# A first stage and a tail written anew in an eight-layer kernel on one core

## The reference, cut to what matters

```python
def _mlstm_cell(q, k, v, ...):            # first layer; q = layernorm(x), k = v = ctx
    ig = einsum('bsf,hf->bsh', concat([q, k, v]), igate_w) + igate_b      # 4 heads
    fg = einsum('bsf,hf->bsh', concat([q, k, v]), fgate_w) + fgate_b
    log_fg = log_sigmoid(fg);  cs = cumsum(log_fg)                        # over 64 tokens
    log_D = cs - shifted(cs).T + ig.T, below the diagonal, else -inf
    D = exp(log_D - rowmax);   C = (q @ k.T / sqrt(32)) * D
    h = C / (max(abs(rowsum(C)), exp(-rowmax)) + 1e-8) @ v
    return (h - mean(h)) / sqrt(var(h) + 1e-5) * (1 + out_w)

def quantize_a16(x):                      # last layer: one scale for the whole tensor
    scale = 32767.0 / max(abs(x))
    return clip(round(x * scale), -32768, 32767) / scale
out = quantize_a16(gelu(quantize_a16(x) @ W_in + b_in)) @ W_out + b_out
```

## Time and profile before

| | us |
|---|---|
| median of 3 runs | 1141.75 |
| lowest and highest | 1138.97, 1147.09 |
| the profiled execution's own time | 1144.12 |
| its span, first to last instruction | 1142.4 |
| PE busy | 1004.6 (88%) |
| DVE busy | 788.7 (69%) |
| ACT busy | 549.8 (48%) |
| POOL busy | 240.6 (21%) |

### The profile page before, as it was taken

The page is one execution under the profiler, slowest core; times in us unless marked ns, Lnnn a source line. Parts: engine busy times, 40 slices in busy tenths (PEclk is TensorE's granted clock), DMA queues, the critical chain, the costliest instruction groups (busy, mean ns, idle before and its releaser), DMA issues.

```text
span 1142.4 us, 33229 instructions
## 1 busy us (share of the span) xinstructions
PE 1004.6 (88%) x12392; PEld 805.7 (71%) x12392; DVE 788.7 (69%) x1883; ACT 549.8 (48%) x1051; POOL 240.6 (21%) x253
## 2 busy tenths in 40 slices
PE   5688999988999997899989999988999988878778
PEld 4457888865777775678867877766778776555536
DVE  6476776566777777455487677657776678887767
ACT  1224444553666553434355656545556553444533
POOL 4474222121233220323010000000000012234300
PEclk9968999998999998899999999999999999999979
DMA  9300000000000000000000000000000000000001
GB/s 368 133 2 1 0 0 0 1 1 3 1 0 0 0 0 1 1 1 0 1 2 1 0 0 0 2 2 2 0 0 0 1 1 1 1 1 0 1 1 37
DMA packets 5924, 16.20 MB, mean 14 GB/s; under 512 B 729, under 2 KB 4962, under 8 KB 5218
## 3 DMA queue, kind: packets, MB, share of 16 engines
q1 hardware_dynamic: 5858, 15.29, 3.4%
HBM read 14.24 MB, written 1.05 MB: 13 GB/s over the span
## 4 chain that ended last, share of the span: by engine, by line
PE 56%; DVE 15%; issue 13%; DVEq 9%; POOL 3%; ACT 3%; POOLq 1%; ACTq 0%
PE banks L1742 8%; PE banks L1815 5%; PE banks L1787 5%; PE banks L1449 4%; PE banks L917 3%; PE banks L1144 3%; PE banks L1775 3%; PE banks L1492 2%; PE banks L1803 2%; PE banks L1364 2%; PE banks L1566 2%; DVE xn L341 1%; PE banks L1479 1%; POOL small L845 1%; PE banks L1532 1%
## 5 line engine op out<-in xcount | busy, mean ns | idle before, releaser
L1750 ACT ACTIVATE work<-banks 128x512 f32<-128x512 f32 x128 | 74.9, 600 | 70.6 <-PE banks L1742 70.6
L363 POOL TENSOR_TENSOR rstd<-var,nhalf 128x2 f32<-128x2 f32 x64 | 45.0, 703 | 297.5 <-DVE var L334 289.8
L1345 ACT ACTIVATE work<-work 128x1024 f32<-128x1024 f32 x64 | 67.9, 1061 | 45.5 <-DVEq L1341 28.1
L1742 PE MATMUL banks<-xT_all,weights 128*128 (+1 forms) x384 | 86.2, 380 | 2.3 <-ACT work L1864 1.8
L1898 DVE TENSOR_TENSOR work<-banks,neg_mask 128x512 f32<-128x512 f32 x64 | 40.7, 685 | 62.4 <-PE banks L1775 60.8
L1742 PEld LDWEIGHTS banks<-xT_all,weights 128*128 128x128 f32 x384 | 71.5, 190 | 13.7 <-ACT work L1864 2.6
L955 ACT ACTIVATE work<-banks,weights 128x256 f32<-128x256 f32 x128 | 53.7, 473 | 55.8 <-PE banks L907 54.9
L1371 ACT ACTIVATE work<-banks 128x512 f32<-128x512 f32 x128 | 67.7, 604 | 13.9 <-PE banks L1364 7.9
L1815 PEld LDWEIGHTS banks<-weights,work 128*128 128x128 f32 x512 | 58.4, 191 | 14.8 <-ACT work L1864 14.8
L917 PE MATMUL banks<-weights,work 128*128 128x128 f32 x512 | 63.1, 276 | 4.8 <-DVE work L1035 4.4
L917 PEld LDWEIGHTS banks<-weights,work 128*128 128x128 f32 x512 | 60.9, 191 | 9.0 <-ACT work L955 7.6
(11 more groups left out here) (341 smaller groups left out, 2301.4 us busy)
## 6 DMA issues: line engine op xcount, KB each, us to landing
weights<-wpack SPq DMA_DIRECT2D x1, 5381.5 KB, 31.4
weights<-wpack SPq DMA_DIRECT2D x1, 2060.0 KB, 12.4
weights<-wpack SPq DMA_DIRECT2D x1, 2049.0 KB, 16.8
weights<-wpack SPq DMA_DIRECT2D x1, 1160.5 KB, 19.1
x_all<-x_in SPq DMA_DIRECT2D x2, 512.0 KB, 4.8
ctxT_all<-ctxT_in SPq DMA_DIRECT2D x1, 1024.0 KB, 6.2
out<-x_all SPq DMA_DIRECT2D x8, 128.0 KB, 1.8
rows<-rows_in SPq DMA_DIRECT2D x1, 832.0 KB
```

Source lines behind the costliest of these rows:

```text
L1345: act.activation(sm[:, u, :], sm[:, u, :], ACT.Exp, scale=scale).then_inc(h["exp"].sem, 1)
L1742: ins = pe.matmul(bank(ring.bank(f"qk{c}"))[:, j * PT:(j + 1) * PT], wt[:, 2 * (c % 4) + j, :], cols(src, p), start=True, stop=True)
L1750: act.activation(dst.rearrange("p c t -> p (c t)"), bank(ring.bank(f"qk{c}")), ACT.Copy) \
```

## The change

**Opening.** The gate weights are spread over 128 stationary columns (`gate_rows`), eight copies with the rest zero, so that the gates come out as rows, with no turn: 128 x 128 products that add up over eight tiles in one bank. `gates_turned` and its copy go. The row work is done in two halves of 128 columns, the first beside the gates of the later pairs. On GpSimd two roots stand ahead of the identity, and `headmask` and the iotas come later; VectorE takes all statistics before it normalises.

**Pass.** ScalarE makes the queries of pairs 2 to 7 (two activations of 128 x 256 each), GpSimd all `spread`s before the pass. On TensorE `heads(p)` stands ahead of `values`, `exponents` and `products` of p + 1. On VectorE `decayed(p + 2)` comes after `scale(p)`, where `decayed(p + 1)` came before `sums(p)`. The list of units is arg0 qa0 qb0 n0 arg1 qa1 qb1 n1 and so on.

**Tail.** The last heads are issued in two halves, the first ahead of the second half's turns and after one more `keep_busy`; the residual constants and the maxima are spread over VectorE's waits; the maximum over the partitions goes through a TensorE transpose, a VectorE maximum and a TensorE product with ones. GpSimd runs a `partition_all_reduce` on data that nobody reads, then the second real one as before.

The diff, cut to its core:

```diff
-        lstm = stage(scans[0] + sum(((scans[p + 1] if p + 1 < PAIRS else []) + [(f"n{p}", "v")] for p in range(PAIRS)),
-                                    []), 1, shift=4)
+        lstm = stage(sum((scans[p] + [(f"n{p}", "v")] for p in range(PAIRS)), []), 1, shift=4)
 
...
+            def gates_spread():
+
+                v.wait_ge(weights_in[0], 16)
+                gw = w("gates").rearrange("p (k a h) -> p k a h", k=3, h=4)
+                for k in range(2):
+                    own = gate_rows[:, 1024 * k:1024 * k + 1056].rearrange("p (t x) -> p t x", x=132)[:, :, 0:P] \
+                        .rearrange("p t (a x) -> p t a x", x=32)[:, :, :, 0:4]
+                    part = gw[:, k:k + 1, :, :].to_broadcast([P, 8, 4, 4])
+                    if k == 0:
+                        v.tensor_copy(own, part)
+                    else:
+                        v.tensor_tensor(own, part, gw[:, 2:3, :, :].to_broadcast([P, 8, 4, 4]), ALU.add) \
+                            .then_inc(gates_merged, 1)
+
...
+            for c in range(4):
+                stats(c)
             apply(0)
             apply(1)
-            stats(3)
-            for p in range(2, PAIRS):
-                apply(p)
...
+            gates_spread()
+            apply(2)
+            apply(3)
+            selectors()
+            apply(4)
+            apply(5)
+            magnitudes(0)
+            apply(6)
+            scans(0)
+            apply(7)
+            magnitudes(1)
+            scans(1)
+
+        def gates_taken_by(act, f):
+
+            here = slice(P * f, P * f + P)
+            act.wait_ge(gates_filled, f + 1)
+            act.activation(lstm_z[:, here], gates_banks[f][64:P, 0:P], ACT.Identity, bias=w("gate_bias")[64:P, 1:2])
+            act.activation(lstm_ig[:, here], gates_banks[f][0:64, 0:P], ACT.Identity, bias=w("gate_bias")[0:64, 0:1]) \
+                .then_inc(rows_taken, 1)
+
+        def logarithms_by(act, f):
+
+            here = slice(P * f, P * f + P)
+            act.wait_ge(abs_made, f + 1)
+            act.activation(lstm_e[:, here], lstm_e[:, here], ACT.Exp, scale=-1.0)
+            act.drain()
+            act.activation(lstm_e[:, here], lstm_e[:, here], ACT.Ln, bias=1.0).then_inc(ln_made, 1)
 
...
                 act.activation(cols(xT_all, p), turn_banks[p % 2], ACT.Copy).then_inc(xt_stored, 1)
-                if p in (4, PAIRS - 1):
-                    f = p // 5
-                    act.wait_ge(gates_filled, f + 1)
-                    act.activation(lstm_t[:, P * f:P * f + P], gates_banks[f][:, 0:P], ACT.Copy) \
-                        .then_inc(gates_taken, 1)
+                if p == 4:
+                    gates_taken_by(act, 0)
+                if p == 5:
+                    logarithms_by(act, 0)
+            gates_taken_by(act, 1)
...
                 pe.wait_ge(xt_stored, p + 2)
                 for u in range(2):
                     f, t = (2 * p + u) // 8, (2 * p + u) % 8
                     for k in range(2):
-                        bk = gates_banks[f][:, 0:P].rearrange("p (g d t h) -> p g d t h", g=2, d=2, t=8)
-                        ins = pe.matmul(bk[:, :, :, t, :],
+                        ins = pe.matmul(gates_banks[f][:, 0:P], gate_rows[:, 1024 * k + P * t:1024 * k + P * t + P],
                                         (ctxT_all if k else xT_all)[:, PT * p + P * u:PT * p + P * u + P],
-                                        gw[:, k, :, :, :], start=(k == 0), stop=(k == 1))
+                                        start=(t == 0 and k == 0), stop=(t == 7 and k == 1))
                 if p % 4 == 3:
                     ins.then_inc(gates_filled, 1)
...
-            pe.wait_ge(m_made, 1)
-            for f in range(2):
-                ins = pe.transpose(em_bank[:, 32 * f:32 * f + 32], lstm_m[0:32, P * f:P * f + P], ident[0:32, 0:32])
-            ins.then_inc(em_filled, 1)
             for p in range(PAIRS):
+                if p in (0, 2):
+                    f = p // 2
+                    pe.wait_ge(m_made, f + 1)
+                    pe.transpose(em_bank[:, 32 * f:32 * f + 32], lstm_m[0:32, P * f:P * f + P], ident[0:32, 0:32]) \
+                        .then_inc(em_filled, 1)
+                heads(p)
                 if p + 1 < PAIRS:
                     values(p + 1)
-                    if p == 0:
-                        pe.wait_ge(em_made, 1)
                     exponents(p + 1)
                     products(p + 1)
-                heads(p)
...
+            def queries(p):
+
+                act.wait_ge(xt_stored, p + 2)
+                act.wait_ge(inputs_used, p)
+                for h in range(2):
+                    act.activation(lstm_q[p % 2][:, h, :], cols(xT_all, p), ACT.Copy, scale=qmask[:, h:h + 1])
+                act.drain().then_inc(staged, 1)
+
...
+                if p == 2:
+                    maxima(1)
                 if p + 1 < PAIRS:
                     values(p + 1)
                     if p >= 1:
                         act.wait_ge(*s.emptied(0, f"qb{p - 1}"))
                     decay(p + 1)
+                if p + 2 < PAIRS:
+                    queries(p + 2)
...
             decayed(0)
+            converts()
+            decayed(1)
             for p in range(PAIRS):
                 v.drain()
-                if p + 1 < PAIRS:
-                    decayed(p + 1)
                 sums(p)
                 if p >= 1:
                     residual(p - 1)
-                elif p == 0:
+                else:
                     masks()
                 scale(p)
+                if p + 2 < PAIRS:
+                    decayed(p + 2)
+                elif p + 2 == PAIRS:
+                    v.tensor_scalar(neg_mask[:], mask_u8, -NEG, None, ALU.mult)
                 if p >= 1:
                     ending(p - 1)
...
             queries(0)
+            spread(0)
             queries(1)
-            spread(0)
             spread(1)
+            constants()
             selectors(0, 4, 8)
             selectors(1, 0, 8)
+            for p in range(2, PAIRS):
+                spread(p)
             g.wait_ge(ow_made, 1)
             for p in range(PAIRS):
-                if p + 2 < PAIRS:
-                    queries(p + 2)
-                    spread(p + 2)
                 g.wait_ge(*hvar_made.at(p, 1))
                 g.tensor_tensor(lstm_hq, lstm_ht, nhalf[:, 0:8], ALU.pow).then_inc(hroot_made.sem, 1)
...
+                if ring is s.epi:
+                    keep_busy(pe, 5, 1)
+                    pe.wait_ge(*ring.emptied(i, "p01"))
+                    heads(ring, i, p, "o_last", (0,))
+                    settle(pe)
...
+            early = T - 2 * PT
+            v.wait_ge(xt_stored, LAST - 1)
+            v.tensor_reduce(amax[:, 4:5], xT_all[:, 0:early], AX, ALU.max, apply_absolute_value=True)
             end3[1](v, s, PAIRS - 2)
             v.drain()
-            end3[2](v, slice(0, TILES - 2))
+            v.tensor_reduce(amax[:, 5:6], xn[:].rearrange("p u d -> p (u d)"), AX, ALU.max, apply_absolute_value=True)
             divided(s.epi, 0, "o_last")
+            end3[2](v, slice(0, TILES // 2))
             end3[0](v, s, PAIRS - 1)
+            end3[2](v, slice(TILES // 2, TILES - 2))
             end3[1](v, s, PAIRS - 1)
 
 
...
-            keep_busy(pe, 5, 3)
+            pe.wait_ge(amax_asked, 1)
+            pe.transpose(amax_row, amax[:, 0:1], ident[:]).then_inc(amax_turned, 1)
+            pe.wait_ge(amax_found, 1)
+            pe.matmul(amax_spread, ones[:], amax[0:1, 1:2], start=True, stop=True).then_inc(amax_turned, 1)
+            keep_busy(pe, 5, 2)
...
-            early = T - PT
-            v.wait_ge(xt_stored, LAST)
-            v.tensor_reduce(amax[:, 4:5], xT_all[:, 0:early], AX, ALU.max, apply_absolute_value=True)
-            v.wait_ge(xt_stored, LAST + 1)
-            v.tensor_reduce(amax[:, 5:6], xT_all[:, early:T], AX, ALU.max, apply_absolute_value=True)
             v.drain()
-            v.tensor_reduce(amax[:, 0:1], amax[:, 4:6], AX, ALU.max).then_inc(amax_asked, 1)
+            v.tensor_reduce(amax[:, 6:7], xn[:].rearrange("p u d -> p (u d)"), AX, ALU.max, apply_absolute_value=True)
+            v.drain()
+            v.tensor_reduce(amax[:, 0:1], amax[:, 4:7], AX, ALU.max).then_inc(amax_asked, 1)
+            v.wait_ge(amax_turned, 1)
+            v.reduce_max(amax[0:1, 1:2], amax_row, AX)
+            v.drain().then_inc(amax_found, 1)
             end3[2](v, slice(TILES - 2, TILES))
-            v.wait_ge(amax_given, 2)
+            v.wait_ge(amax_turned, 2)
+            v.tensor_copy(amax[:, 1:2], amax_spread)
+            v.drain()
             scales(v, amax[:, 1:2], amax[:, 2:3], amax[:, 3:4], 32767.0)
...
-            g.wait_ge(amax_asked, 1)
-            g.partition_all_reduce(amax[:, 1:2], amax[:, 0:1], P, ABSMAX).then_inc(amax_given, 1)
+            g.wait_ge(q_ready.sem, 2)
+            g.partition_all_reduce(amax[:, 7:8], nhalf[:, 0:1], P, ABSMAX).then_inc(amax_given, 1)
...
```

(5 more changed lines are left out.)

198 lines of the change are left out of this document (95 added, 103 removed).

## The result

| | before | after |
|---|---|---|
| median of the runs | 1142.6 us (1138.97 to 1147.09) | 1167.56 us (1167.36 to 1169.67) |
| ratio after / before | | 1.0213, 95% interval 1.019 to 1.0236 |
| profiled execution, its span, granted clock | 1144.12, 1142.4, 0.969 | 1167.66, 1165.9, 0.947 |
| last turn ahead of the second stage | 91.54 | 118.97 |
| first rounding | 1102.18 | 1124.28 |

The prediction was 1134.0; the kernel became 25 us slower. All of that arises in the first stage, whose last turn comes 27.4 us later. The tail gives 2.7 us back and the stages between 1.2, which leaves the 23.5 us between the spans of the two profiled executions.

A forecast was written before the change was run, and what follows sets the result against it. It took the middle as dense on TensorE (56% of the last-ending chain) and VectorE's list as setting the first stage's pairs. First stage 3.4 plus tail 4.2 is 7.6 us off the median 1141.75, so 1134; range 1125 to 1144.

The forecast's parts named there:

- The pass, a pair: First stage: cost of one pair, with VectorE's chain 5.8 us at the higher clock and TensorE late at the lower, 7.85.
- GpSimd's first root at 10.15: Opening: the code load ahead of GpSimd's first named instruction stands behind no wait, so its start stays at 10.15 us.
- Gates end near 30.4: Opening: gates end between 29.2 (higher clock level) and 31.5 (lower), taken as 30.4 us, against 31.5 before.
- my 5.9 less 4.1: Opening: TensorE's last turn queues behind VectorE's scans and `apply(7)`, about 5.9 us, with 4.1 covered by other gates.
- First `decayed` at 35.9 (34.7 to 37.0): End of the opening: gates' end 30.4 plus 0.1 plus 5.4 of row work gives 35.9 us, against 42.35 before.
- Pair of 5.8 at the higher and 7.85 at the lower level, mixture 6.7: First stage's pass: pair time by clock level, against 6.43 us before; half the time at each level gives 6.7; chance 0.55.
- A new wait of products(p+2) for scale(p), through the bank of `n(p)`: Pass: `qa(p+2)` takes the bank of `n(p)`, so products, then `decayed(p+2)`, wait for the scale; within the 5.8 us pair.
- The turn at 88.2 (80.9 to 96.6): Last turn ahead of the second stage: 88.2 us, 3.4 earlier; clock all high 80.9, all low 96.6.
- Pair time will depend on the clock: Pass: pair time, before independent of TensorE's clock, becomes 5.8 us at granted clock 1.00 and 7.85 at 0.50.
- Tail 4.2 (3.2 to 5.5): Last heads to first rounding: heads 1.1 us earlier, `ending` to first rounding 2.9 less, sum 4.0, taken as 4.2.
- Rival 2: Pass: clock stays low, products wait behind heads, values and exponents on every pair; 1.9 us more, 1144; chance 0.13.
- The chances: Whole kernel: mixture 0.55, high 0.24, low 0.13, load or row work 0.08; faster by over 1% 0.31, within 0.67, slower 0.02.

The follow-up runs named there:

- e1: The changed kernel with waits that ask for the number at which VectorE really empties each unit, all else kept; 1140.45 us, ratio 0.9981 to the kernel before.
- e3: The kernel before with only the new list of units and the new TensorE order; 1166.57 us, ratio 1.0227 to the kernel before.
- e3b: The kernel before with the new list and TensorE order, but waits on VectorE's real counts; 1145.73 us, ratio 1.0026 to the kernel before.
- e2: The changed kernel with the old list of units and the old order on TensorE; 1128.43 us, ratio 0.9881 to the kernel before.
- e9: As e1, with each turn issued behind the next pair's heads instead of ahead of them; 1141.82 us, ratio 0.9993 to the kernel before.
- e10: As e9, with banks of its own for each kind of unit in the first stage; 1137.46 us, ratio 0.9962 to the kernel before.
- e4: The kernel before with the changed tail alone; 1138.74 us, ratio 0.9959 to the kernel before.
- e7: As e2, with `apply(7)` ahead of the first half's scans on VectorE; 1126.26 us, ratio 0.9836 to the kernel before.
- e15: The kernel before with only the query products of pairs 2 to 7 moved from GpSimd to ScalarE; 1141.31 us, ratio 0.9988 to the kernel before.
- e13: As e2, with the query products of pairs 2 to 7 on GpSimd ahead of its power; 1132.54 us, ratio 0.9897 to the kernel before.

## Why the prediction was wrong

**The step that failed** is in "The pass, a pair": "TensorE is in time there: turn to products 69.06 - 67.23 = 1.83 plus heads 1.05 is 2.9, and the scale is done after 3.6." I let the heads start as soon as the turn ahead of them was done, so I cost their wait at nothing. I had computed bank numbers from the new list (`qa(p+2)` is unit 4(p+2)+1) but not the counts that the same list gives to the waits. The real term is scale(p-1) to heads(p), 0.48, in place of `decayed(p)` to heads(p): it puts heads, values, exponents, products, `decayed`, `ending`, sums and power in one row, 11.1 us a pair instead of the 6.7 of the sum, and 27.1 us in all (after against e1; 20.8 on the kernel before, e3 against e3b).

Point by point:
- *GpSimd's first root at 10.15*: 10.77, idle for 9.44 instead of 8.83. Right in that nothing made it wait for data; 0.6 off.
- *Gates end near 30.4*: ScalarE takes them at 32.05. The stall of TensorE's last turn that I named is there, but 3.67 long where my 5.9 less 4.1 made it 1.8, and the last gates ran at the lower level (the turn at 27.91 took 0.69). The upper bound of 31.5 is missed by 0.5.
- *First `decayed` at 35.9 (34.7 to 37.0)*: 38.15 in after, 36.98 in e1, 37.16 in e2. The row work took 6.1 (32.05 to 38.15), inside my 4.5 to 6.5; the gates are what was late.
- *Pair of 5.8 at the higher and 7.85 at the lower level, mixture 6.7*: in after 11.1. With the count mended: 5.84 at the higher level, 7.44 and 7.30 in the two pairs whose heads, values and exponents ran at the lower one (both e9), and 7.79 wholly at the lower level (e1). The sizes hold for the kernel that I had in mind; the mean was 7.12 in e1, because its level was low for more than half of the pass (0.69).
- *A new wait of products(p+2) for scale(p), through the bank of n(p)*: with a count that names the scale it exists, is seen in e9 and gone in e10. In after its count is too low to hold anything, and the heads' wait stands in for it.
- *The turn at 88.2 (80.9 to 96.6)*: 118.97; e1 93.53, inside. 5.3 off there: 1.1 by `decayed(0)`, 2.1 by five pairs, 0.8 by the last one (6.18, not 5.4), the rest by the first pairs.
- *Pair time will depend on the clock*: after has no pair wholly at the higher level to show it. The one wholly at 0.50 took 11.18, the other four, at 0.65 to 0.66, took 10.89 to 11.39. How much of the 11.1 the lower level makes is not shown. With mended counts the pair does depend on it, as said above (e9).
- *Tail 4.2 (3.2 to 5.5)*: 4.1 by the first rounding, near the 4.2, though by two errors that cancel (0.7 for the heads, not 1.1; 3.4 behind `ending`, not 2.9). Behind it 1.4 is given back in after and about 0.9 in e4, which leaves 2 to 3 in the runs. I had noted that `keep_busy` ends 0.8 late and left it out of the sum; it was 0.9.
- *Rival 2*, the only one that pointed to slower, had the right idea (products behind heads, values and exponents) and a price of 1.9 us. *The chances* gave 0.02 to slower by over 1%, because no rival asked whether the waits still name what they mean.

The Trainium skill ("GPSIMD Engine Reference", 4.1 Engine selection) sends a reduction along partitions to GpSimd. Here the trace goes against that for the first such call only. From VectorE's last maximum to the first step of the scale it was 3.14 us in before (1097.96 to 1101.10), with the end of the 5.74 us of idle time ahead of GpSimd's first call in it, and 1.83 in after by way of TensorE (1121.70 to 1123.53). The second call of before needed 0.67 (1119.50 to 1120.17), so there GpSimd is the quicker way, which agrees with the rule. The idle time did not go, it moved: in after 7.04 us of it lie ahead of the call at 1127.43, where nothing waits for it. Of the 3.4 us that the tail wins behind `ending`, 1.3 are this step and 1.7 the maxima over the free dimension, which are done earlier; whether those would have gained anything with GpSimd's first call behind them, no run shows.

The Trainium skill ("TensorE: Matmul & The Clock Gate", Part 1: The HAM clock gate) holds that activity releases the low clock and that idleness brings it back. The trace of after agrees: behind each of its idle times of 3.0 to 5.4 us the heads took 1.92, where they take 1.12 at the higher level. In four of the five pairs the level came back near the end of TensorE's row of work (1.00 from 77 to 80, for one), where only products and a turn were left; in the third it did not. The mixture that I forecast, against that rule taken alone, is what the runs with mended counts show: 0.69 in e1, 0.82 in e9.

**To carry to other kernels.** When a wait is a number on a counting semaphore and the number is worked out from a list, a change of that list is a change of every such wait: write down, for two or three waits, which operation of the engine that counts reaches the number, in that engine's own order. A count that comes too late is silent, since the result stays right and only the releaser in brackets tells. A count that comes too early, as that of `n(p)` here, is as silent while another wait happens to cover it, so whoever mends the first alone lays the second bare; e1 mends both. And of two waits that end close together, taking away one may show nothing; here, by the traces, turn and bank each hid the other.

**What I had not expected of the chip.** GpSimd and VectorE slow each other in other pairs of operations than `ending` and the product: in e7 a spread that takes 0.60 took 2.65 beside the 2.27 us `neg_len`:

```profile
36.63 2.27 DVE L813 TENSOR_TENSOR neg_len<-iseq,lensf 128x2048 f32<-128x2048 f32 x1
36.72 2.65 POOL L869 TENSOR_TENSOR work<-work,tsel 32x256 f32<-32x256 f32 x1 [0.18 <-issue]
```

And the scatter differs by kernel. Over ten executions e9 (1137.85 to 1147.32), e10 (1133.35 to 1142.97) and e15 (1139.54 to 1147.14) spread over 8 to 10 us, and before over 11 in twenty-five (1138.88 to 1149.91), while e1 and e4 stay within 4 us in ten each. What sets it is not known; the spreading ones are not those with one order, list or opening in common. (e2, e3 and e13 stay within 3.5 us, but in four executions each, which says less.)
